# A routed feed-forward layer on one core: the two expert results of a token laid side by side in memory, and read by one transfer per group

## The reference, cut to what matters

```python
probs = sigmoid(xt @ gate_w.T + gate_b)            # xt: 3584 tokens x 256
w, idx = top_k(probs, 2);  w = w / (sum(w) + 1e-8)
ge = sum(one_hot(idx, 6) * w[..., None], axis=1)
for e in range(6):                                 # only two of the six terms of a token aren't zero
    y = y + ge[:, e:e+1] * ((silu(xt @ ew1[e].T) * (xt @ ew3[e].T)) @ ew2[e].T)
z = (silu(xt @ fc1.T) * (xt @ fc2.T)) @ fc3.T      # the shared expert, for every token
x = x + y + z
```

## Time and profile before

| | |
|---|---|
| median of 3 runs | 1488.41 us |
| lowest and highest of them | 1482.65 and 1497.91 us |
| the profiled execution: time | 1486.21 us |
| the profiled execution: span | 1484.4 us |
| mean granted TensorE clock | 0.951 |

### The profile page before, as it was taken

How to read it: one execution, slowest core, us unless ns; L and a number is a source line. 1 busy time by engine, 2 the same in 40 slices (tenths; PEclk the granted TensorE clock), 3 DMA queues, 4 the chain that set the end, 5 groups by cost and what they waited for, 6 DMA issues and landing times.

```text
span 1484.4 us, 34511 instructions
## 1 busy us (share of the span) xinstructions
PE 1310.8 (88%) x11121; PEld 1170.5 (79%) x11121; DVE 912.0 (61%) x2926; ACT 656.1 (44%) x1526; POOL 524.6 (35%) x716
## 2 busy tenths in 40 slices
PE   5999999999897599999999999999999877888976
PEld 4888998898787578888888888888888766777865
DVE  4676567567545366667666776677676465444546
ACT  3534434334332154555455545555555552444531
POOL 3223223224312422442344334433343642233344
PEclk9999999999998799999999999999999987999987
DMA  7699100000002445455545555456554231223367
GB/s 184 154 239 237 42 0 0 0 0 0 15 6 60 108 103 140 112 118 130 121 112 124 130 132 116 109 134 134 121 129 116 78 114 52 83 83 90 102 157 197
DMA packets 134974, 151.39 MB, mean 102 GB/s; under 512 B 41235, under 2 KB 118404, under 8 KB 134868
## 3 DMA queue, kind: packets, MB, share of 16 engines
q1 hardware_dynamic: 128148, 134.55, 39.0%
q0 software_dynamic: 6160, 15.69, 3.3%
q10 hardware_dynamic: 576, 0.07, 0.0%
HBM read 79.27 MB, written 45.82 MB: 84 GB/s over the span
## 4 chain that ended last, share of the span: by engine, by line
PE 60%; issue 12%; DVE 8%; SPq 5%; DMA 5%; POOL 4%; ACT 3%; DVEq 0%; ACTq 0%; POOLq 0%
PE psum L863 17%; PE psum L1105 6%; PE psum L1272 5%; PE psum L1139 4%; PE psum L1120 4%; SPq L490 3%; PE psum L1125 3%; DMA qst<-negm 3%; PE psum L1292 2%; PE psum L984 2%; PE psum L970 2%; PE psum L981 2%; PE psum L1075 2%; PE psum L852 1%; PE psum L1315 1%
## 5 line engine op out<-in xcount | busy, mean ns | idle before, releaser
L2139 DVE CUSTOM_DVE_ANT_0 junk<-psum,biasq 112x375 f32<-112x375 f32 x512 | 277.1, 545 | 170.7 <-issue 135.1
L1621 ACT ACTIVATE pr<-psum 125x448 f32<-125x448 f32 x384 | 205.0, 545 | 127.0 <-PE psum L1125 121.8
L1125 PE MATMUL psum<-qst,kst 97*125 97x224 f32 x768 | 234.3, 354 | 0.0
L1105 PE MATMUL psum<-kst,qst 96*112 96x376 f32 x512 | 187.8, 372 | 19.9 <-DVE smax L2139 17.5
L1120 PE MATMUL psum<-flagk,negbig 125*125 125x448 bf16 x384 | 140.6, 366 | 14.4 <-DMA qst<-negm 9.9
L1125 PEld LDWEIGHTS psum<-qst,kst 97*125 97x125 f32 x768 | 147.1, 192 | 7.0
L699 POOL TENSOR_TENSOR rs<-rs,neg_half 112x1 f32<-112x1 f32 x32 | 18.2, 570 | 343.9 <-DVE rs L2052 343.9
L1105 PEld LDWEIGHTS psum<-kst,qst 96*112 96x112 f32 x512 | 92.8, 182 | 44.1 <-DVE smax L2139 35.3
L828 POOL DMA_INDIRECT routed_y<-yb,yrow x61 | 59.1, 969 | 139.1 <-ACT yb L1792 130.6
L1139 PE MATMUL psum<-pr,vaug 125*32 125x112 f32 x3072 | 96.6, 267 | 0.7 <-ACT pr L1621 0.7
L1139 PEld LDWEIGHTS psum<-pr,vaug 125*32 125x32 f32 x3072 | 72.0, 111 | 17.1 <-issue 11.6
(11 more groups left out here) (306 smaller groups left out, 3551.1 us busy)
## 6 DMA issues: line engine op xcount, KB each, us to landing
kst<-khi SPq DMA_DIRECT2D x64, 376.0 KB, 6.9
routed_h<-in_route_pad SPq DMA_DIRECT2D x6, 3640.0 KB
kst<-klo SPq DMA_DIRECT2D x32, 376.0 KB, 9.2
ctxT<-in_ctxT SPq DMA_DIRECT2D x32, 375.0 KB, 6.0
hblk<-routed_h SPq DMA_DIRECT2D x61, 130.0 KB, 2.1
qst<-qhi SPq DMA_DIRECT2D x128, 56.0 KB, 4.0
stage<-in_e SPq DMA_DIRECT2D x21, 256.0 KB, 3.2
maskq<-in_mask SPq DMA_DIRECT2D x32, 164.1 KB
```

Source lines behind the costliest of these rows:

```text
L1105: pe.matmul(bank[max_bank(n, hd)][0:T, 0:S2E], head(qst[par][0:ROWS], hd), pair(kst[par][0:ROWS], hd // 2), start=True, stop=True).then_in ...
L1125: mm = pe.matmul(bank[q % 3][0:KP, cols(i, 2 * T)], pair(kst[par], n)[:, cols(q // HPB, KP)], both(qst[par], n), start=False, stop=True, s ...
L1621: nc.scalar.activation(pr[q % PROBS][:].rearrange("k i q -> k (i q)"), bank[q % 3][0:KP, 0:GT], ACT.Exp, scale=1.0 / HD ** 0.5).then_inc(s ...
L2139: nc.vector.tensor_tensor_reduce(out=junk[:, hd % 2, :], in0=bank[max_bank(n, hd)][0:T, 0:S2], in1=biasq[:, par, :], scale=1.0, scalar=-3e ...
```

## The change

A token's two results now lie in neighbouring rows of `routed_y`: result r of token n in row 2 * n + r. The token's number in C_TOKEN is therefore kept doubled (`tokens` and its step are multiplied by TOP = 2), and `output_rows` adds the 0 or 1 of `mine` in place of 0 or CAP. A group's 2 x 448 rows are then one region, and `load_products` reads it by one transfer, a piece of which is 2 KB (both results of one token), where there were two transfers of 1 KB pieces. The ring of four places takes the same room in the two weight tiles, but a place holds both results next to each other: places 0 and 1 are in `e13_hi`, 2 and 3 in `e13_lo`. `add_products` and `add_routed` read (and `add_products` writes) blocks of 256 numbers that stand 512 apart. The wait of `add_products` counts one transfer in place of two.

```diff
-    tokens = ((np.arange(RB)[None, :] - RB) * T + row).astype(np.float32)
+    tokens = (TOP * ((np.arange(RB)[None, :] - RB) * T + row)).astype(np.float32)
...
-            products = [[e13[r][:].bitcast(F32).rearrange("p e c w n -> p (e c w n)")[0:T, n * GB * D:(n + 1) * GB * D].rearrange("t (j d) -> t j d", j=GB)
-                         for n in range(RINGS)] for r in range(TOP)]
+            products = [e13[n // 2][:].bitcast(F32).rearrange("p e c w n -> p (e c w n)")[0:T, n % 2 * GB * TOP * D:(n % 2 + 1) * GB * TOP * D].rearrange("t (j r d) -> t j r d", j=GB, r=TOP)
+                        for n in range(RINGS)]
...
-                for r in range(TOP):
-                    src = ybuf[r * CAP + g * GT:r * CAP + (g + 1) * GT, :].rearrange("(j t) d -> t j d", j=GB)
-                    sp.dma_start(products[r][g % RINGS], src).then_inc(s3[f"first_in{g % RINGS}"], 16)
+                src = ybuf[TOP * g * GT:TOP * (g + 1) * GT, :].rearrange("(j t r) d -> t j (r d)", j=GB, r=TOP)
+                sp.dma_start(products[g % RINGS].rearrange("t j r d -> t j (r d)"), src).then_inc(s3[f"first_in{g % RINGS}"], 16)
...
-                nc.gpsimd.tensor_scalar(told(par, C_TOKEN), told(par, C_TOKEN), float(RB * T), None, ALU.add).then_inc(s3["gating"], 1)
+                nc.gpsimd.tensor_scalar(told(par, C_TOKEN), told(par, C_TOKEN), float(TOP * RB * T), None, ALU.add).then_inc(s3["gating"], 1)
...
-                pool.wait_ge(s3[f"first_in{n}"], 16 * TOP * (g // RINGS + 1))
-                nc.gpsimd.tensor_tensor(products[0][n], products[0][n], products[1][n], op=ALU.add).then_inc(s3["both"], 1)
+                pool.wait_ge(s3[f"first_in{n}"], 16 * (g // RINGS + 1))
+                nc.gpsimd.tensor_tensor(products[n][:, :, 0], products[n][:, :, 0], products[n][:, :, 1], op=ALU.add).then_inc(s3["both"], 1)
...
-                nc.vector.tensor_tensor(x[:, group(g), :], x[:, group(g), :], products[0][g % RINGS], op=ALU.add).then_inc(s3["x_new"], 1)
+                nc.vector.tensor_tensor(x[:, group(g), :], x[:, group(g), :], products[g % RINGS][:, :, 0], op=ALU.add).then_inc(s3["x_new"], 1)
...
-                nc.vector.scalar_tensor_tensor(out=yrow[:, u:u + 1], in0=mine, scalar=float(CAP), in1=told[:, C_TOKEN:C_TOKEN + 1], op0=ALU.mult, op1=ALU.add).then_inc(s4["meta"], 1)
+                nc.vector.scalar_tensor_tensor(out=yrow[:, u:u + 1], in0=mine, scalar=1.0, in1=told[:, C_TOKEN:C_TOKEN + 1], op0=ALU.mult, op1=ALU.add).then_inc(s4["meta"], 1)
```

## The result

| | before | after |
|---|---|---|
| median of 22 runs each | 1488.44 us | 1479.57 us |
| lowest to highest | 1478.38 to 1498.48 | 1472.47 to 1496.41 |
| ratio, 95% interval | | 0.9945 [0.9923, 0.9967] |
| profiled execution | 1486.21 | 1476.38 |
| its span, granted clock | 1484.4, 0.951 | 1474.5, 0.959 |

The account below looks back on a forecast made before the run. The prediction held the end bound first by the rate of the `routed_y` transfers, and by their order. Terms 0 + 0 - 1.8 + 0 = -1.8 us gave a median of 1486.6 us from 1488.41, range 1478 to 1494.

Parts of the forecast that it names:

- within 1%: Whole kernel: the change moves the time by no more than 1% (14.9 us) either way; chance 0.96.
- the fast rival: End reads: larger pieces run at 305 GB/s and TensorE's clock may stay up, together -6.3 us, 1482; chance 0.17.
- Row numbers, doubled token numbers, scatters: Before the end: same instructions, shapes and bytes, only another constant, so 0 us.
- Eight issues fewer: SP at the end: four issues replace the four reads' eight; 0 us, with up to 0.5 us to be had.
- 2 KB pieces at 245 GB/s, landing 0.7 earlier: End reads: 245 GB/s in place of 234, so `load_turned(7)` lands 0.7 us earlier, at 1448.6.
- nothing moves: Rival for the end reads: old pieces remain or the rate doesn't depend on the piece; 1488.4 us, chance 0.2.
- The far ends: Bounds for the rate of the end reads: 305 GB/s if much faster, 211 if slower.
- Which engine is second waits: End, POOL and DVE: POOL comes first, its group 7 part takes 2.06 us, not 3.17; `add_products(3)` ends 1.8 us earlier.
- Strided additions: POOL and DVE at the end: additions over blocks of 256 numbers, 512 apart, cost 0 us.
- The upper end of 3.7: DVE at the end: most the strides could cost, 1.22 us more on each of three additions on the chain.
- Wrong in kind if a scatter's landing shows up among the waits of the blocks: Sign for the blocks: the ring of four covers each scatter's landing, so none should appear as a wait.

Follow-up runs that it names:

- e5_rows: The kernel before with the new row numbers alone (doubled token numbers, new rows), old tiles, two transfers a group: 1477.93 us, ratio 0.9937 to before.
- e10_doubled: The kernel before, old rows, with doubled token numbers on POOL, halved in the blocks by one more DVE instruction: 1479.27 us, ratio 0.9899 to before.
- e9_undoubled: e5_rows with its new rows, but undoubled token numbers on POOL, doubled by DVE in the blocks: 1489.83 us, ratio 0.9959 to the kernel before.
- e3_halves: The changed kernel with each 896 KB read cut into two transfers of 2 KB pieces: 1477.83 us, ratio 0.9953 to the kernel before.
- e2_layout: The changed kernel's rows and tiles, but two transfers of 1 KB pieces a group: 1478.10 us, ratio 0.9955 to the kernel before.
- the left: The five kernels, the kernel before among them, whose L725 on POOL has a mean of 947 to 979 ns: median 1489.5 us over 95 executions.
- the right: The nine kernels, the changed one among them, whose L725 on POOL has a mean of 339 to 467 ns: median 1478.3 us over 96 executions.
- e12_late: The kernel before, numbers undoubled, with POOL's addition L718 alone moved behind the subtraction of L728: 1478.40 us, ratio 0.9889 to before.

## Why the prediction was right, and where its steps were not

*The direction, the range and "within 1%"* held: 1479.57 in 1478 to 1494. That is luck in good part. The range's lower end came from the fast rival (1482) and 4 us for a median's scatter, and neither is what happened; the direction was forecast from the end, and most of the gain came from the loop. The sum was off by 7 us, and the step that failed is the first: "*Row numbers, doubled token numbers, scatters.* Same instructions, same shapes, same bytes, another constant: 0." Priced at nothing, it holds the gain: e5_rows has it with this step alone (0.9937), e10_doubled with its doubled numbers alone (0.9899), and in e9_undoubled the old meeting on POOL is back when they go (979 ns). The step counted instructions and bytes, and took for granted that instructions of the same shape last as long as before. They meet those of another engine, and here 0.11 us of shift decided which instruction of POOL was caught, and for how long. The prediction used the Trainium skill's exclusive lock (SBUF — State Buffer, Who interferes with whom) for the end alone; the rows of 0.31 and 1.08 us agree with it in the loop too. On DVE's side the loop shows less than a full block: the subtraction took 0.98 us and not 0.94 where L724 had begun 0.08 us ahead of it.

*Eight issues fewer: 0.* Nothing speaks against it: e3_halves has them back at 0.9953. The four issues took 2.47 us, where "within some 2 us" was forecast.

*2 KB pieces at 245 GB/s, landing 0.7 earlier.* The rate of 237 to 243 is near it, but single profiles of 2 KB pieces gave 218 to 243, and the landing moved by 0.16 us. The rival "nothing moves", the rate doesn't depend on the piece, describes the transfers better; with e2_layout at 0.9955, no part of the result is seen to hang on them. The far ends, 305 and 211 as rates of the reads alone, didn't occur.

*Which engine is second waits: -1.8.* Half right. POOL's part did fall from 3.17 to 2.13 and DVE's addition did wait in its place, as the exclusive lock named in the prediction has it. What the sum left out is the next meeting: DVE's addition, begun 0.29 us behind POOL's, was stretched to 1444.86, and so reached into `add_products(3)` of 1443.74, which took 3.37 in place of the 2.33 entered. "DVE waits instead, where it has time" was the error: a blocked DVE is late, and blocks POOL in turn. That the end is 1.4 shorter all the same comes mostly from TensorE's stretch behind it, at a higher granted clock, and 1.4 is no more than the kernels of one side differ by (57.8 to 60.1 for the 2 KB pieces). So the 1.8 us forecast and the 1.4 measured agree by luck; no run shows that the change shortened the end.

*Strided additions: 0.* Right: POOL's alone take 2.33 us and DVE's alone 1.22, as before. The upper end of 3.7 wasn't needed.

*Blocks.* "Wrong in kind if a scatter's landing shows up among the waits of the blocks" was no usable sign: it does show up, for DVE's L2368, with 1.8 us in 4 waits before and 0.6 us in 2 after. So the ring of four doesn't cover every landing, but the new rows made nothing worse, as expected. The blocks are 174.3 us in two kernels of before and 173.9 to 176.3 in the rest, without a pattern that an experiment explains.

**What stays open.** Why L718 with 672.0 starts 0.11 us sooner behind L708 than with 336.0: there are 0.27 us between their starts before (766.20 and 766.47) and 0.16 after (760.91 and 761.07), in every such kernel, and no run shows the cause. How the 0.4 us a row passes to TensorE isn't followed to the end. Between 600 and 1120 us TensorE's waits for a named releaser add up to 29.8 to 32.6 us on the left and 24.3 to 29.2 on the right; those for `klo` stay (6.4 to 6.8), and what differs is mostly the wait for the transfer of `negm` into `qst`, 23.1 to 25.8 us in four kernels of the left and 10.5 to 22.2 on the right. In the kernel before it is 8.9, with 12.8 for DVE's `smax` beside it. Why POOL's sooner end shortens that isn't shown. Nor is it shown whether the higher clock on the right, which goes with about half of the difference, comes of a TensorE that is fed more evenly.

## What to carry to other kernels

Where GpSimd and VectorE work side by side in a loop, an edit of one small GpSimd instruction can change the time by more than the edit's purpose: after any change compare the mean durations of small instructions in the stages that it wasn't meant to touch. Split a change into its halves before crediting its idea; here the half that nobody would have timed held most or all of the gain. Between kernels 0.5% apart, take the clock's share out of the times before a cause is given all of the gain. And when a lock turns in one engine's favour, carry the delay of the other one on to its next meeting.

## What was not expected of the hardware

- An instruction of 112x6 on GpSimd took 0.31 us alone and 1.08 us when a VectorE subtraction of 128x750 had begun 0.03 us before it; its mean over 24 rows was 947 ns, and 339 in the changed kernel.
- The constant and numbers of one GpSimd addition (336.0 or 672.0, both float) set 0.11 us of its start, in all five kernels with the one and all eight with the other at the same place; moving the addition (e12_late) had the same effect on the time as doubling it.
- Reads from HBM on one queue ran at 222 to 237 GB/s in pieces of 1 KB and at 218 to 243 in pieces of 2 KB; the two sizes overlap.
